# The first conditioning stage of a two-layer network, rewritten: which engine does what, and in what widths

## The reference

```python
tf = sigmoid(sum(time_emb, -1))
decay = exp(-exp(w)) * (0.5 + 0.5 * tf)          # one number per channel and batch
ek = exp(minimum(k, 30.0)); ekv = ek * v
# a[t] = a[t-1] * decay + ekv[t],  b[t] = b[t-1] * decay + ek[t]
nf, df = scan(ekv, ek); nb, db = scan(ekv, ek, reverse=True)
euk = exp(minimum(u + k, 30.0))
num = nf + nb - ekv + euk * v
den = df + db - ek + euk
out = sigmoid(r) * num / maximum(den, 1e-8) * (0.8 + 0.2 * tf)
```

## Time and profile before

| what | value |
|---|---|
| runs | 1446.56, 1454.03, 1455.33 us; median 1454.03 |
| profiled execution | span 1444.4 us from first to last instruction; the page gives no other time for it |
| first stage | 0 to 81.9 us; the first matmul starts at 82.60 |
| DVE busy from 9.1 to 81.9 us | 71.4 of 72.8 us |
| POOL busy in the same stretch | 37.1 us |
| PE busy from 82.0 us to the end | 1208.5 of 1362.4 us |

### The profile page before, as it was taken

One profiled execution on the slowest core, in us unless ns is written; L12 is line 12 of the kernel. 1 busy time (PEld: TensorE's weight loads), 2 busy tenths in 40 slices (PEclk: granted clock), 3 DMA queues, 4 the chain that ended last, 5 costly groups with the idle time before them and its releaser, 6 DMA issues. The chain is left out here.

```text
span 1444.4 us, 16409 instructions
## 1 busy us (share of the span) xinstructions
PE 1208.4 (84%) x4614; PEld 641.6 (44%) x4614; DVE 879.5 (61%) x1244; ACT 593.9 (41%) x1742; POOL 569.6 (39%) x531
## 2 busy tenths in 40 slices
PE   0048899779897699999986898988799787997998
PEld 0014444334453344444434555643485336844443
DVE  7978999389985564246325948729741496504222
ACT  2025454454454232232224546647672476711110
POOL 5562675626665231002002856727651275500000
PEclk9999999999999799999998999989899898997999
DMA  6000000000003400000003000030000000000000
GB/s 253 0 22 1 0 1 1 1 0 0 0 0 120 157 0 1 0 0 0 33 10 136 1 1 0 0 138 1 1 2 1 1 0 0 0 0 8 0 0 29
DMA packets 5481, 33.24 MB, mean 23 GB/s; under 512 B 528, under 2 KB 1936, under 8 KB 3536
## 3 DMA queue, kind: packets, MB, share of 16 engines
q1 hardware_dynamic: 5424, 32.61, 5.8%
HBM read 31.56 MB, written 1.05 MB: 23 GB/s over the span
## 5 line engine op out<-in xcount | busy, mean ns | idle before, releaser
L813 POOL TENSOR_TENSOR decays<-decays,scores 128x768 f32<-128x768 f32 x64 | 124.8, 1953 | 152.0 <-ACT decays L749 152.0
L575 PE MATMUL pg<-h,weights 128*128 (+1 forms) x136 | 66.5, 612 | 85.5 <-PEq L356 82.6
L1998 POOL TENSOR_TENSOR f_pair<-m,weights 128x256 f32<-128x256 f32 x80 | 90.9, 1156 | 92.6 <-DVE m L2019 91.6
L1101 PE MATMUL ph<-h,weights 128*128 x256 | 116.5, 600 | 0.0
L1406 POOL TENSOR_TENSOR prob_latent<-prob_latent,inverse_latent 128x128 f32<-128x128 f32 (+1 forms) x128 | 81.5, 660 | 70.4 <-DVE inverse_latent L1396 70.1
L575 PE MATMUL px<-h,weights 128*128 x136 | 73.3, 664 | 26.1 <-DVE conv L886 26.0
L749 ACT ACTIVATE decays<-pcum,neg_cum 128x256 f32<-128x256 f32 (+1 forms) x256 | 87.7, 449 | 11.4 <-PE pcum L628 11.2
L1246 DVE TENSOR_TENSOR mid<-up,ph 128x512 f32<-128x512 f32 x44 | 30.2, 687 | 98.5 <-ACT up L1158 98.5
L1406 POOL TENSOR_TENSOR prob_gqa<-prob_gqa,inverse_gqa 128x128 f32<-128x128 f32 (+1 forms) x128 | 62.0, 506 | 58.4 <-DVE inverse_gqa L1396 56.8
L1158 ACT ACTIVATE up<-ph 128x512 f32<-128x512 f32 x44 | 26.3, 597 | 140.4 <-PE ph L1101 140.4
L886 DVE SCALAR_TENSOR_TENSOR conv<-px,pp,conv 128x510 f32<-128x510 f32 (+2 forms) x102 | 75.1, 737 | 14.5 <-ACT conv L714 11.6
(11 more groups left out here) (327 smaller groups left out, 3069.6 us busy)
## 6 DMA issues: line engine op xcount, KB each, us to landing
weights<-in_w_mixer SPq DMA_DIRECT2D x2, 2048.0 KB, 18.3
weights<-in_w_moe SPq DMA_DIRECT2D x2, 1536.0 KB, 7.8
moe_rest<-in_w_moe SPq DMA_DIRECT2D x2, 1536.0 KB, 13.9
weights<-in_w_gqa SPq DMA_DIRECT2D x1, 3072.0 KB, 10.2
weights<-in_w_gqa SPq DMA_DIRECT2D x1, 2048.0 KB, 14.7
weights<-in_w_moe SPq DMA_DIRECT2D x1, 1920.0 KB, 9.1
weights<-in_w_mixer SPq DMA_DIRECT2D x1, 1536.0 KB, 11.8
weights<-in_w_moe SPq DMA_DIRECT2D x1, 1152.0 KB, 11.7
```

The lines of the kernel that those rows point to most:

```text
L575: op = nc.tensor.matmul(out[0:m, :], w[:, col + k * m:col + (k + 1) * m], net.h[:, ds(i * PAIR + k * TOK, TOK)], start=(k == 0), stop=(k = ...
L813: nc.gpsimd.tensor_tensor(decays[:, head % 4], decays[:, head % 4], scores[:], ALU.mult).then_inc(decay_scaled, 1)
L1101: op = nc.tensor.matmul(out[:], wt[:, n * D + k * P:n * D + (k + 1) * P], net.h[:, ds(i * PAIR + k * TOK, TOK)], start=(k == 0), stop=(k = ...
L1998: op = nc.gpsimd.tensor_tensor(out[:, :, s, :], src[:, :, 1 - s, :], sin[:, None, s, :].to_broadcast([P, 4, HALF]), ALU.mult)
```

## The change

Only conditioning 0 in `stage_condition` is rewritten; the other three still use `CondUnit`, with their turns counted from 0 now instead of from 2. ACT issues the DMA of `pp` itself, ahead of its table load, and SP begins with `f`. ACT writes the decay rows, four instructions of 128x256 for a pair, the second pair's into the buffer `f_pair`, so that the pairs have a buffer each. The scans of den read `e` where it lies, and the copies `e_pair` and `f_pair` go. DVE takes e * f, euk - e and own * f over from POOL, and all its sums, products, bounds and the reciprocal run over 1028 columns at once; the scans stay in halves. POOL keeps the two sums num + num_b and num + own. The second pair's `euk` = min(f + u, 30) is put ahead of the first pair's reciprocal. The core of the diff:

```diff
         def _(sp):
-            sp.dma_start(net.pp[:], dram["pp"]).then_inc(net.params_loaded, 16)
...
-            pool.wait_ge(net.consts_made, 1)
             nc.gpsimd.memset(net.f[:].rearrange("p (r t) -> p r t", t=SEG)[:, :, 0:1], 0.0) \
                 .then_inc(pads_ready, 1)
-            nc.gpsimd.memset(net.decay[:].rearrange("p (r t) -> p r t", t=SEG)[:, :, 0:1], 0.0) \
-                .then_inc(pads_ready, 1)
-
-            pool.wait_ge(cols_ready, 3)
+            for decay in decays:
+                nc.gpsimd.memset(decay[:].rearrange("p (r t) -> p r t", t=SEG)[:, :, 0:1], 0.0) \
+                    .then_inc(pads_ready, 1)
             for pair in range(PAIRS):
-                pool.wait_ge(e_padded, pair + 1)
-                unit.pool_operands(pair, pair)
-                for step in unit.pool_numerator(pair):
-                    step()
+
+                pool.wait_ge(scanned, pair + 1)
+                nc.gpsimd.tensor_tensor(net.num[:], net.num[:], net.num_b[:], ALU.add) \
+                    .then_inc(num_made, 1)
+                pool.wait_ge(num_made, 2 * pair + 1)
+                pool.wait_ge(own_made, 2 * pair + 2)
+                nc.gpsimd.tensor_tensor(net.num[:], net.num[:], net.ev_pair[:], ALU.add) \
+                    .then_inc(num_made, 1)
 
         @block.scalar
         def _(act):
+            act.dma_start(net.pp[:], dram["pp"]).then_inc(net.params_loaded, 16)
...
-            for pair in range(PAIRS):
+
+            def make_decay(pair):
+
+                for k in range(KT):
+                    for b in range(BB):
+                        row = (k * BB + b) * SEG
+                        at = k * BATCH + pair * BB + b
+                        nc.scalar.activation(
+                            decays[pair][:, row + 1:row + SEG],
+                            net.ones[:, 0:1].to_broadcast([P, SEQ]), ACT.Copy,
+                            scale=net.dcol[:, at:at + 1]).then_inc(decay_made, 1)
+
+            def exp_e(pair):
                 e = net.e[:, pair * UNIT:(pair + 1) * UNIT]
                 act.wait_ge(min_ready, pair + 1)
-                nc.scalar.activation(e, e, ACT.Exp).then_inc(e0_exp, 1)
-            unit.scalar(0, 0)
+                nc.scalar.activation(e, e, ACT.Exp).then_inc(e_exp, 1)
+
+            def exp_shifted(pair):
+                act.wait_ge(shifted, pair + 1)
+                nc.scalar.activation(net.euk[:], net.euk[:], ACT.Exp).then_inc(shifted_exp, 1)
+
+            act.wait_ge(cols_ready, 3)
+            act.wait_ge(net.consts_made, 1)
+            make_decay(0)
+            exp_e(0)
+            exp_shifted(0)
+            exp_e(1)
+            make_decay(1)
             tanh_h()
-            unit.scalar(1, 1)
+            exp_shifted(1)
...
+            def shift(pair):
+
+                for k in range(KT):
+                    cols = slice(k * BB * SEG, (k + 1) * BB * SEG)
+                    op = v.tensor_scalar(
+                        net.euk[:, cols],
+                        net.f[:, pair * UNIT + k * BB * SEG:pair * UNIT + (k + 1) * BB * SEG],
+                        net.pp[:, PP_U + k:PP_U + k + 1], 30.0, ALU.add, ALU.min)
+                op.then_inc(shifted, 1)
+
+            def pad_e(pair):
+                e = net.e[:, pair * UNIT:(pair + 1) * UNIT].rearrange("p (r t) -> p r t", t=SEG)
+                dve.wait_ge(e_exp, pair + 1)
+                v.memset(e[:, :, 0:1], 0.0).then_inc(e_padded, 1)
+                dve.wait_ge(e_padded, pair + 1)
+
+            def scan(out, pair, data, reverse):
+                for k in range(KT):
+                    here = slice(k * BB * SEG, (k + 1) * BB * SEG)
+                    order = slice(None, None, -1) if reverse else slice(None)
+                    op = v.tensor_tensor_scan(
+                        out[:, here][:, order], decays[pair][:, here][:, order],
+                        data[:, here][:, order], 0.0, ALU.mult, ALU.add)
+                return op
+
+            bound_e(0)
+            shift(0)
+            bound_e(1)
             for pair in range(PAIRS):
-                e = net.e[:, pair * UNIT:(pair + 1) * UNIT].rearrange("p (r t) -> p r t", t=SEG)
-                dve.wait_ge(e0_exp, pair + 1)
-                v.memset(e[:, :, 0:1], 0.0).then_inc(e_padded, 1)
-            dve.wait_ge(e_padded, PAIRS)
-            for pair in range(PAIRS):
-                for step in unit.vector(link, pair, pair):
-                    step()
+                e = net.e[:, pair * UNIT:(pair + 1) * UNIT]
+                f = net.f[:, pair * UNIT:(pair + 1) * UNIT]
+                pad_e(pair)
+                dve.wait_ge(decay_made, (pair + 1) * KT * BB)
+                scan(net.den, pair, e, False)
+                scan(net.den_b, pair, e, True)
+                link(v.tensor_tensor(net.ev_pair[:], e, f, ALU.mult))
+                scan(net.num, pair, net.ev_pair, False)
+                scan(net.num_b, pair, net.ev_pair, True).then_inc(scanned, 1)
+                dve.wait_ge(scanned, pair + 1)
+                dve.wait_ge(shifted_exp, pair + 1)
+                v.tensor_tensor(net.euk[:], net.euk[:], e, ALU.subtract).then_inc(own_made, 1)
+                dve.wait_ge(own_made, 2 * pair + 1)
+                v.tensor_tensor(net.ev_pair[:], net.euk[:], f, ALU.mult).then_inc(own_made, 1)
+                link(v.tensor_tensor(net.den[:], net.den[:], net.den_b[:], ALU.add))
+                link(v.tensor_tensor(net.den[:], net.den[:], net.euk[:], ALU.add))
+                link(v.tensor_scalar(net.den[:], net.den[:], 1e-8, None, ALU.max))
+                if pair + 1 < PAIRS:
+                    shift(pair + 1)
+                link(v.reciprocal(net.den[:], net.den[:]))
+                dve.wait_ge(num_made, 2 * (pair + 1))
+                for b in range(BB):
+                    num = net.num[:].rearrange("p (k b t) -> p k b t", **shape)[:, :, b, 1:SEG]
+                    den = net.den[:].rearrange("p (k b t) -> p k b t", **shape)[:, :, b, 1:SEG]
+                    m = net.m[:, pair * PAIR:(pair + 1) * PAIR].rearrange(
+                        "p (k b t) -> p k b t", **shape)
+                    op = v.scalar_tensor_tensor(m[:, :, b, :], num,
+                                                net.scol[:, pair * BB + b:pair * BB + b + 1],
+                                                den, ALU.mult, ALU.mult)
+                link(op)
                 make_h(pair)
...
-                        unit.scalar(i, i + PAIRS)
+                        unit.scalar(i, i)
...
```

More of the change, by code:

```diff
@@ L344, in stage_condition @@
     sem = net.sem
-    e0_exp, e_padded = sem("e0_exp"), sem("e_padded")
+    e_exp, e_padded = sem("e_exp"), sem("e_padded")
     min_ready = sem("min_ready")
@@ L349, in stage_condition @@
     pads_ready, links = sem("pads_ready"), sem("cond_links")
+    decay_made, shifted, shifted_exp = sem("decay_made"), sem("shifted"), sem("shifted_exp")
+    scanned, own_made, num_made = sem("scanned"), sem("own_made"), sem("num_made")
     net.cond_sems = [sem(n) for n in ("u_ready", "euk_ready", "operand_ready", "scans_done",
@@ L352, in stage_condition @@
                                          "num_steps")]
-    unit = CondUnit(net, 0, net.cond_sems)
     tanh_h, make_h, _ = condition_input(net, "_mixer")
+    decays = (net.decay, net.f_pair)
+    shape = dict(k=KT, b=BB)
     with nc.Block() as block:
@@ L424, in _, with bound_e @@
                 ALU.mult).then_inc(cols_ready, 1)
-            dve.wait_ge(pads_ready, 2)
-            for pair in range(PAIRS):
+            dve.wait_ge(pads_ready, 3)
+            def bound_e(pair):
                 unit_cols = slice(pair * UNIT, (pair + 1) * UNIT)
@@ L828, in _ @@
             with nc.gpsimd.Fori(0, PAIRS) as i:
-                unit.pool_operands(i, i + PAIRS)
-                numerator = list(unit.pool_numerator(i + PAIRS))
+                unit.pool_operands(i, i)
+                numerator = list(unit.pool_numerator(i))
                 for b in range(BB):
@@ L955, in _ @@
                 link = Links(dve, links, i, MIXER_LINKS)
-                cond = unit.vector(link, i, i + PAIRS)
+                cond = unit.vector(link, i, i)
                 taps(i, 0, link)
@@ L1057, in stage_moe @@
         unit = CondUnit(net, cond, net.cond_sems) if cond is not None else None
-        turn0 = PAIRS * cond if cond is not None else 0
+        turn0 = PAIRS * (cond - 1) if cond is not None else 0
         tanh_h, make_h, h_ready = prepare or (lambda: None, lambda: None, None)
@@ L1634, in _ @@
                     if u == 4:
[L1635 removed]
+                        unit.scalar(i, i + 2 * PAIRS)
             nc.scalar.preload_act_table_set("exp_and_others")
@@ L1643, in _ @@
             with nc.gpsimd.Fori(0, PAIRS) as i:
-                unit.pool_operands(i, i + 3 * PAIRS)
-                numerator = list(unit.pool_numerator(i + 3 * PAIRS))
+                unit.pool_operands(i, i + 2 * PAIRS)
```

(1 more changed line is left out.)

2 lines of the change are left out of this document (1 added, 1 removed).

## The result

The changed kernel takes 1437.59 us in the median of seven runs (1435.59 to 1443.05), the kernel before 1450.99 us in the median of seven (1445.09 to 1458.49). The ratio is 0.9914, with a 95% interval of 0.989 to 0.9939: faster by a little under 1%. The forecast was 1440.0 us.

A forecast was written before the change was run, and what follows sets the result against it. The first stage, bound by DVE's queue taking turns with POOL, stands whole in the time. Pad at 8.68, two pairs 58.44 and a shift 0.72 end it at 67.84 instead of 81.83: 14.0 us less, 1440.0 us, range 1431 to 1447.

The forecast's parts named there:

- DVE's queue is the chain: First stage: DVE's queue sets its length, and is long because DVE and POOL operations take turns, each keeping the other out.
- Rival 2: Whole-width operations leave POOL's two sums until DVE's reciprocal: 8.8 us more go, 1431 us; chance 0.05.
- One pair: From a pair's first scan to its gate's end, DVE's operations and waits for POOL sum to 29.1 us.
- The mis-sized term: Whole-width reciprocal on DVE in each pair: taken as 6.3 us, between bounds of 5.9 and 6.66 us.
- The head: Up to the first scan: load 0.44 us earlier at 7.98, e's bound to 8.68, pad and its wait 0.12.
- 1.4 us of cover: Head: ACT's rows and exp end at 7.3 us, so pp may land 1.4 us later without delaying the first scan.
- The sign that `pp` lands before 4.5 us: Head, among the things that would show the forecast: the DMA of pp lands before 4.5 us.
- Rival 1: Small costs add up: DVE's waits on itself cost 0.13 us, load not earlier, reciprocals 6.66: 2.9 us more, 1442.9 us; chance 0.10.
- rival 3: SP's loads are served ahead of ACT's, pp lands at 26.5 us, first scan 30.4: 7.7 us more, 1461.7 us; chance 0.02.
- DVE's lead over POOL at the scans' end: After the num scans of a pair: DVE's euk - e starts 0.1 us ahead of POOL's first sum.

The follow-up runs named there:

- pp_sync: The changed kernel with the DMA of pp back on SP's queue ahead of f; second gate ends at 68.78 us instead of 68.37.
- all_dve: The changed kernel with POOL's two sums of num on DVE behind the reciprocal; gate ends at 64.94 us instead of 68.37, median 1438.69 us, ratio 0.9913.
- own_pool: The changed kernel with euk - e and own * f back on POOL in whole width; second gate ends at 69.97 us instead of 68.37.
- ef_pool: The changed kernel with the product e * f back on POOL in whole width; second gate ends at 70.11 us instead of 68.37.
- halves: The changed kernel with DVE's sums, products and bound in halves and the reciprocal in eight pieces; second gate ends at 69.86 us instead of 68.37.
- hide_sums: The changed kernel with POOL's sums released by the bound, second pair's shift ahead of it; gate 60.29 us instead of 68.37, median 1431.47 us, ratio 0.9865.
- hide_three_timed: POOL's sums beside the reciprocal, own * f on POOL there too, second pair's shift behind it; against the kernel before: gate 59.00 us, median 1431.58 us, ratio 0.9881.

## Why the prediction was right, point by point

**DVE's queue is the chain and its busy time is mostly turns: shown.** The two POOL sums moved by one semaphore took 8.08 us out of the stage (68.37 to 60.29) with no operation removed. Rival 2, that the wide operations leave POOL's sums to the reciprocal by themselves, did not come true; made so by hand, it is worth 8.1 of the 8.8 us that it was priced at.

**One pair: 29.1 us forecast, 29.37 measured** (39.00 to 68.37). The sums and products fell as worked out: own * f and den + euk 3.26 us each, the others 1.2. The scans, factor and gate were right to 0.1 us. The mis-sized term is the reciprocal: 6.58 us, not 6.3. The slope between 8 and 128 columns with its start-up gave 6.39, and I went below it towards the pieces' 5.9; the truth lay by the pieces' total of 6.66, so the whole width is worth 0.08 us there. Twice the missing 0.28 us is the 0.53 us by which the stage ended later than forecast (68.37 against 67.84).

**The head: right at the end, wrong on the way.** The pad was forecast for 8.68 and came at 8.68, by luck: I had the second load of `f` in front (7.98), and ACT with 1.4 us of cover. In the trace the load was there by 7.58, `pp` was 1.25 us later, and ACT's four rows (1.70 us against 1.48) and exp set the time; the two errors cancelled. The sign that `pp` lands before 4.5 us failed (4.69). `pp_sync` shows what the move is worth, 0.41 us, close to the 0.44 of the forecast, and by another way: 1.21 us lost on `pp`, over 0.8 us won on `f`. On the rule of the Trainium skill (DMA: Bandwidth & Descriptors, Issuing engines are not separate DMA queues): that `pp` comes later beside `f` agrees with the interleaving. That only the issuing time is saved doesn't: the second `f` was waited for until 8.43 in `pp_sync` and not at all at 7.58 here (nor at 7.26 in `all_dve`), so it landed 0.85 us or more sooner for an issue 0.44 us earlier. Whether the queue or the order of the issues does it stays open: no run has `pp` on SP's queue behind `f`.

**What each part is worth.** Undone one at a time, the difference and own * f cost 1.60 us, the product 1.74, the decay rows 2.30, the widths 1.49, the DMA 0.41: 7.5 of the 13.46 us, if they add up, which no run shows. The rest was not undone alone. Rows of the kernel before, not among those above, show a large piece of it, the shift beside POOL's product and copy in the second pair:

```profile
46.22 3.38 POOL L194 TENSOR_TENSOR ev_pair<-e,f 128x1028 f32<-128x1028 f32 x1 [8.40 <-DVE m L317]
47.32 4.61 DVE L263 TENSOR_SCALAR euk<-f,pp 128x514 f32<-128x514 f32 x2
49.57 2.08 POOL L196 TENSOR_TENSOR e_pair<-e,ones 128x1028 f32<-128x1028 f32 x1
```

The shift lasts 0.89 us in the changed kernel, where no POOL operation stands beside it:

```profile
28.86 0.89 DVE L465 TENSOR_SCALAR euk<-f,pp 128x514 f32<-128x514 f32 x2
```

The missing copies `e_pair` and `f_pair` were not tried by themselves.

**The stage's gain in the time.** 13.46 us left the stage, 13.4 the median. The forecast took its 14.0 us off the median of three runs, 1454.03; off the median of seven it would have been 1437.0, so most of the 2.4 us between 1440.0 and 1437.59 is the scatter of those three. The range also held rivals 1 and 2: the time alone would not have told them from the forecast, the rows do. In the two profiled executions only 11.0 left the span: from the gate to the end they took 1362.6 us before and 1365.0 after. That need not be the change, since executions of one program differ by more. The two experiments whose gates end within 0.14 us of each other, `own_pool` and `ef_pool`, have the same program behind it and differ by 14.2 us there, 1376.9 and 1362.7. They ran on two chips; `halves`, on the chip of `own_pool` and with a gate 0.11 us sooner, took 1368.2, so 8.7 us of it need no second chip. The rows of span and granted clock of `own_pool` and `ef_pool`:

```profile
core 0: 1446.9 us, clock 0.944
```

```profile
core 0: 1432.8 us, clock 0.953
```

Over the 23 runs of the kernel before that stand beside `hide_sums` and `hide_three_timed`, all on one chip, the span less 81.83 us goes from 1355.5 us (clock 0.953) to 1374.6 (clock 0.944). PE's granted clock lies at the lower of its two levels, 1.2 GHz, in more or fewer stretches of one and the same program: from 250 to 480 us its mean is 0.93 of full speed in `own_pool` and 0.95 in `ef_pool`. This scatter hides the 3.4 us of `all_dve`, and it is why a ratio of 0.9914 has an interval of half a per cent. Whether a stage that ends sooner also lengthens the rest a little stays open: the medians of the span less the gate are 1366.7 us for the changed kernel, 1368.8 for `hide_sums`, 1371.7 for `all_dve` and 1370.2 for `hide_three_timed`, against 1368.2 (beside `hide_sums` and `all_dve`) and 1364.3 (beside `hide_three_timed`) for the kernel before. All three experiments lie above the kernel before, by 0.6, 3.5 and 5.9 us, while the changed kernel's median fell by as much as its stage. That leans towards a rest that lengthens under a still shorter stage, without showing it.

Rival 1 (1442.9 us) and rival 3 (`pp` starves) did not come: DVE's waits on itself cost 0.03 to 0.05 us throughout, and `pp` landed at 4.69. Of rival 1 only the reciprocal's 6.66 us came near (6.58).

## What to carry to other kernels

A busy engine is not a working one: where a DVE instruction of a known size lasts much longer in one place, subtract the end of the POOL operation beside it. If what is left is about its own duration (1.08 of 1.23 us here), the two take turns, and moving an operation of 1028 columns to POOL cost DVE 2.1 us to save 1.2 (`ef_pool`). Put POOL's work beside operations that take no turns, here the reciprocal; the order by one semaphore gave 8 us, more than any part of the rewrite (13.5 us in all) that was undone alone.

## What was not expected of the hardware

- With `pp` on ACT's queue and `f` on SP's, both issued at 0.74 us, the second `f` was there 0.85 us or more earlier, though `f` was issued only 0.44 us earlier; `pp` came 1.2 us later.
- The reciprocal's time hardly depends on its pieces or on POOL: 6.57 us for 1028 columns in one instruction, 6.67 in eight, 6.58 with POOL at work beside it.
- DVE's lead over POOL at the scans' end is 0.05 us (49.36 against 49.41), half of what the forecast had; DVE still began first in both pairs.
